# A quantized layer: GpSimd rounds gate, sigmoid and half of act, TensorE spreads the largest value

## The reference

```python
def act_qdq(x):                       # 16 bits, one step for the whole tensor
    qmax = 2.0 ** 15 - 1.0
    scale = jnp.maximum(jnp.max(jnp.abs(x)) / qmax, 1e-12)
    return jnp.clip(jnp.round(x / scale), -qmax - 1.0, qmax) * scale

def fixed_qdq_u16(x):
    scale = 1.0 / 65536.0
    return jnp.clip(jnp.round(x / scale), 0.0, 65535.0) * scale

x = act_qdq(x)
up = act_qdq(x @ lpbq_dequant(w_up).T)        # weights: 4 bits in blocks of 32
gate = act_qdq(x @ lpbq_dequant(w_gate).T)    # 1024 x 768
sig = fixed_qdq_u16(jax.nn.sigmoid(gate))
gate = act_qdq(gate * sig)                    # "act"
o = act_qdq(gate * up)                        # "hid"
return o @ lpbq_dequant(w_down).T
```

## Time and profile before

| | |
|---|---|
| three runs | 4011.01, 4022.51, 4026.56 us (median 4022.51) |
| profiled execution | 4017.75 us, its span 4016.4 us |
| TensorE busy | 3686.9 us, 92% of the span |
| VectorE | 2754.8 us, 69% |
| ScalarE | 2149.5 us, 54% |
| GpSimd | 1459.3 us, 36% |
| the stage of the change | about 830 to 969 us of the span |

### The profile page before, as it was taken

One profiled execution on the slowest core, in us unless ns is written; L12 is line 12 of the kernel. 1 busy time (PEld: TensorE's weight loads), 2 busy tenths in 40 slices (PEclk: granted clock), 3 DMA queues, 4 the chain that ended last, 5 costly groups with the idle time before them and its releaser, 6 DMA issues. The chain is left out here.

```text
span 4016.4 us, 100168 instructions
## 1 busy us (share of the span) xinstructions
PE 3686.9 (92%) x42032; PEld 3196.3 (80%) x42032; DVE 2754.8 (69%) x7205; ACT 2149.5 (54%) x2963; POOL 1459.3 (36%) x1261
## 2 busy tenths in 40 slices
PE   7999999874999999988999999985988999999857
PEld 6888888643888888857788888864987888888646
DVE  5777777665777777753788888854446777777544
ACT  4566565454656656533455555533644656566444
POOL 3333333101322322130665555414763323222146
PEclk9999999997999999999999999986998999999978
DMA  3122123001111111010211121003542111110035
GB/s 99 51 67 59 51 65 115 25 17 37 47 39 35 42 43 35 10 41 10 79 66 59 51 67 59 26 13 105 204 139 75 35 35 46 39 35 26 13 116 176
DMA packets 125584, 235.80 MB, mean 59 GB/s; under 512 B 9920, under 2 KB 114768, under 8 KB 121296
## 3 DMA queue, kind: packets, MB, share of 16 engines
q1 hardware_dynamic: 118032, 175.58, 14.8%
q0 software_dynamic: 7104, 53.81, 3.8%
HBM read 208.39 MB, written 20.97 MB: 57 GB/s over the span
## 5 line engine op out<-in xcount | busy, mean ns | idle before, releaser
L610 ACT COPY prob_t<-ps 128x1024 f32<-128x1024 f32 x512 | 518.0, 1012 | 1037.3 <-PE ps L498 1037.3
L498 PE MATMUL ps<-c_ident,prob 128*128 128x128 f32 (+1 forms) x6656 | 902.5, 277 | 13.7 <-ACT prob L748 9.9
L498 PEld LDWEIGHTS ps<-c_ident,prob 128*128 128x128 f32 (+1 forms) x6656 | 734.7, 141 | 148.0 <-issue 121.5
L748 ACT ACTIVATE prob<-prob,nmx 128x1601 f32<-128x1601 f32 x512 | 828.8, 1626 | 1.1 <-DVE nmx L661 1.1
L528 PE MATMUL ps<-wv,ctx 128*128 128x256 f32 x4992 | 703.6, 289 | 3.1 <-DVE vals L620 3.1
L514 PE MATMUL ps<-ctx,wk 128*128 128x400 f32 (+1 forms) x3072 | 691.0, 360 | 7.4 <-POOL ctx L810 3.4
L528 PEld LDWEIGHTS ps<-wv,ctx 128*128 128x128 f32 x4992 | 618.7, 186 | 10.0 <-DVE vals L620 4.0
L514 PEld LDWEIGHTS ps<-ctx,wk 128*128 128x128 f32 x3072 | 535.2, 191 | 16.5 <-issue 4.9
L652 DVE CUSTOM_DVE_ANT_0 prob<-ps,mk 128x400 f32<-128x400 f32 (+2 forms) x1024 | 525.8, 569 | 32.4 <-PE ps L486 25.2
L655 DVE TENSOR_SCALAR_CACHE_REDUCE prob<-ps 128x400 f32<-128x400 f32 (+2 forms) x1024 | 525.4, 570 | 11.4 <-PE ps L486 8.9
L682 DVE SCALAR_TENSOR_TENSOR keys<-ps,cols,keys 128x400 fp32r<-128x400 f32 (+2 forms) x384 | 243.6, 634 | 367.7 <-ACT keys L754 360.5
(11 more groups left out here) (352 smaller groups left out, 4242.2 us busy)
## 6 DMA issues: line engine op xcount, KB each, us to landing
raw_ctx<-in_ctx_t SPq DMA_DIRECT2D x120, 400.0 KB, 3.3
raw_ctx<-in_ctx_t SPq DMA_DIRECT2D x60, 402.0 KB, 5.1
raw_ctx<-in_ctx_t SPq DMA_DIRECT2D x60, 399.0 KB, 3.3
mk<-in_mask_f SPq DMA_DIRECT2D x32, 400.2 KB, 5.5
mk<-in_mask_i SPq DMA_DIRECT2D x16, 800.5 KB, 4.4
sorted<-zeros SPq DMA_DIRECT2D x2, 3840.0 KB, 20.2
rows<-sorted SPq DMA_DIRECT2D x30, 256.0 KB, 6.8
done<-done SPq DMA_DIRECT2D x30, 256.0 KB, 2.1
```

The costliest lines, as they stand in the source:

```text
L498: mm = pe.transpose(ps[0:w, turn_bank(u, i) + a, r * P:(r + 1) * P], prob[u % 2][:, r, x * P:x * P + w], cst['ident'][:])
L610: copy(prob_t[0:w, place(2 * i):place(2 * i) + nb, :], ps[0:w, turn_bank(u, i):turn_bank(u, i) + nb, :]).then_inc(st[sem], 1)
L748: a.activation(prob[h % 2][:, r, :], prob[h % 2][:, r, :], ACT.Exp, bias=nmx[:, r:r + 1], accum_out=den[h % 2][:, r:r + 1]).then_inc(st['e ...
```

## The change

The change rewrites who does what in the gate and act sections:

- the integers of gate, now with the step multiplied in (`rounded_rows`), are made by GpSimd for all six tiles, those of act for the odd tiles;
- the second pass of the sigmoid's rounding (`sigmoid_rounded`) is GpSimd's; VectorE keeps the first, and runs one tile ahead: it does the first pass of tile m, then the product and the reduction of tile m-1;
- the products of act with up are GpSimd's for the odd tiles, VectorE's for the even ones;
- the largest over partitions comes from a transpose on TensorE of one column spread over 128 (`spread_largest`), whose row VectorE reduces; `step_size` is split in `step_begun` and `step_made`, and for up the quantization of the down weight stands between the two;
- ScalarE's scalings of up come one tile later among its copies of gate.

```diff
             elif old[0] == 'act':
-                engine.wait_ge(*st.at('hidden', old[1] + 1))
+                engine.wait_ge(*hidden(old[1]))
...
+        def spread_largest(n):
+            pe.wait_ge(*st.at('step_big', names.index(n) + 1))
+            pe.transpose(ps[:, 3, 0:P], one[n][:, 0:1].broadcast_to([P, P]), k.cst['ident'][:]).then_inc(st['step_all'], 1)
...
         for m in range(NF):
             project_act(k, st, gate[:, m:m + 1], (6, 7), 'gate_mm', 'gate_out', first=2 * m)
-            scale_rows('up', m)
+            if m:
+                scale_rows('up', m - 1)
+        scale_rows('up', NF - 1)
         turn(2, 'down')
         for m in range(NF):
             scale_rows('gate', m)
-            integers('gate', m)
             buffer_free(a, ('sig', m))
-            a.wait_ge(*st.at('whole', whole['gate', m]))
-            a.activation(buffer(('sig', m))[:], buffer(('gate', m))[:], ACT.Sigmoid,
-                         scale=one['gate'][:, 2:3]).then_inc(st['sigmoid'], 1)
+            a.wait_ge(*st.at('whole', m + 1))
+            a.activation(buffer(('sig', m))[:], buffer(('gate', m))[:], ACT.Sigmoid).then_inc(st['sigmoid'], 1)
...
+        def rounded_rows(n, m):
+            b = buffer((n, m))
+            p.wait_ge(*st.at('scaled', scaled[n, m]))
+            p.tensor_scalar(b[:], b[:], -BIG, one[n][:, 2:3], ALU.add, ALU.mult).then_inc(st['whole'], 1)
+
+        def sigmoid_rounded(m):
+            sig = buffer(('sig', m))
+            p.wait_ge(*st.at('sig_up', m + 1))
+            p.tensor_scalar(sig[:], sig[:], -BIG / 65536.0, 65535.0 / 65536.0, ALU.add, ALU.min).then_inc(st['sig'], 1)
+
+        for m in range(NF):
+            rounded_rows('gate', m)
+            if m:
+                sigmoid_rounded(m - 1)
+        sigmoid_rounded(NF - 1)
+        for m in range(1, NF, 2):
+            rounded_rows('act', m)
+            p.wait_ge(*st.at('whole', NF + m // 2 + 1))
+            p.tensor_tensor(gate[:, m], buffer(('act', m))[:], up[:, m], ALU.mult).then_inc(st['hidden_pool'], 1)
...
+        def step_made(n):
+            v.wait_ge(*st.at('step_all', names.index(n) + 1))
+            v.tensor_reduce(one[n][:, 1:2], ps[:, 3, 0:P], AX, ALU.max).then_inc(*did.up())
+            v.wait_ge(*did.now())
             v.tensor_scalar(one[n][:, 2:3], one[n][:, 1:2], 1.0 / 32767.0, 1e-12, ALU.mult, ALU.max).then_inc(*did.up())
...
+        for m in range(NF + 1):
+            if m < NF:
+                sig = buffer(('sig', m))
+                v.wait_ge(*st.at('sigmoid', m + 1))
+                v.tensor_scalar(sig[:], sig[:], 0.0, BIG / 65536.0, ALU.max, ALU.add).then_inc(st['sig_up'], 1)
+            if m:
+                v.wait_ge(*st.at('sig', m))
+                v.tensor_tensor(gate[:, m - 1], buffer(('gate', m - 1))[:], buffer(('sig', m - 1))[:],
+                                ALU.mult).then_inc(st['gated'], 1)
+                v.wait_ge(*st.at('gated', m))
+                largest('act', m - 1)
+        step_begun('act')
+        step_made('act')
```

More of the change, by code:

```diff
@@ L1474, in quantized_ffn @@
     quantized = {what: i + 1 for i, what in enumerate(w for w in order if w[0] in ('x', 'up', 'hid'))}
-    whole = {what: i + 1 for i, what in enumerate(w for w in order if w[0] in ('gate', 'act'))}
     tile_of = {'x': xq, 'up': up, 'gate': gate, 'act': gate, 'hid': gate}
@@ L1518, in pe @@
         pe.wait_ge(*st.at('w_turned', 6))
-        project_pe(k, st, turned['gate'], xq, (6, 7), 'gate_mm', 'gate_out')
+        for m in range(NF):
+            for n in range(2):
+                if m:
+                    pe.wait_ge(*st.at('gate_out', 2 * m + n - 1))
+                for c in range(C):
+                    mm = pe.matmul(ps[:, 6 + n, :], turned['gate'][:, c, m * P:(m + 1) * P], xq[:, c, n * 512:(n + 1) * 512],
+                                   start=(c == 0), stop=(c == C - 1))
+                mm.then_inc(st['gate_mm'], 1)
+            if m == 0:
+                spread_largest('up')
         turn(2, 'down')
+        for n in ('gate', 'act', 'hid'):
+            spread_largest(n)
         pe.wait_ge(*st.at('w_turned', 9))
@@ L1545, in turn, with integers @@
                 a.copy(flat[:, 512 * j:512 * j + 512], ps[:, j, :]).then_inc(st['w_turned'], 1)
-        def integers(n, m):
-            a.wait_ge(*st.at('scaled', scaled[n, m]))
-            a.activation(buffer((n, m))[:], buffer((n, m))[:], ACT.Identity, bias=minus_col[:]).then_inc(st['whole'], 1)
+        def integers(m):
+            a.wait_ge(*st.at('scaled', scaled['act', m]))
+            a.activation(buffer(('act', m))[:], buffer(('act', m))[:], ACT.Identity, bias=minus_col[:]).then_inc(st['whole_act'], 1)
         a.wait_ge(*st.at('ln_var', 1))
@@ L1574, in act @@
                 if n == 'hid':
-                    a.wait_ge(*st.at('hidden', m + 1))
+                    a.wait_ge(*hidden(m))
                 scale_rows(n, m)
-                if n == 'act':
-                    integers(n, m)
+                if n == 'act' and m % 2 == 0:
+                    integers(m)
     def pool():
         p = nc.gpsimd
-        for i, n in enumerate(names):
-            p.wait_ge(*st.at('step_big', i + 1))
-            p.partition_all_reduce(one[n][:, 1:2], one[n][:, 0:1], P, RMAX).then_inc(st['step_all'], 1)
+        def rounded_rows(n, m):
[6 more added lines that the diff above has]
+            p.tensor_scalar(sig[:], sig[:], -BIG / 65536.0, 65535.0 / 65536.0, ALU.add, ALU.min).then_inc(st['sig'], 1)
+        for m in range(NF):
+            rounded_rows('gate', m)
[6 more added lines that the diff above has]
+            p.tensor_tensor(gate[:, m], buffer(('act', m))[:], up[:, m], ALU.mult).then_inc(st['hidden_pool'], 1)
     def dve():
@@ L1614, in dve @@
                             apply_absolute_value=True).then_inc(*did.up())
-        step_size('x')
+        step_begun('x')
+        step_made('x')
         for c in range(C):
@@ L1629, in dve @@
             largest('gate', m)
-        step_size('gate')
-        for m in range(NF):
-            sig = buffer(('sig', m))
-            v.wait_ge(*st.at('sigmoid', m + 1))
-            v.tensor_scalar(sig[:], sig[:], 0.0, BIG / 65536.0, ALU.max, ALU.add).then_inc(*did.up())
-            v.wait_ge(*did.now())
-            v.tensor_scalar(sig[:], sig[:], -BIG / 65536.0, 65535.0 / 65536.0, ALU.add, ALU.min).then_inc(*did.up())
-            v.wait_ge(*did.now())
-            v.scalar_tensor_tensor(gate[:, m], buffer(('gate', m))[:], one['gate'][:, 2:3], sig[:], ALU.mult,
-                                   ALU.mult).then_inc(st['gated'], 1)
-            v.wait_ge(*st.at('gated', m + 1))
-            largest('act', m)
-        step_size('act')
-        for m in range(NF):
-            v.wait_ge(*st.at('whole', whole['act', m]))
-            v.scalar_tensor_tensor(gate[:, m], buffer(('act', m))[:], one['act'][:, 2:3], up[:, m], ALU.mult,
-                                   ALU.mult).then_inc(st['hidden'], 1)
-            v.wait_ge(*st.at('hidden', m + 1))
+        step_begun('gate')
+        step_made('gate')
+        for m in range(NF + 1):
[3 more added lines that the diff above has]
+                v.tensor_scalar(sig[:], sig[:], 0.0, BIG / 65536.0, ALU.max, ALU.add).then_inc(st['sig_up'], 1)
+            if m:
+                v.wait_ge(*st.at('sig', m))
[5 more added lines that the diff above has]
+        step_made('act')
+        for m in range(NF):
+            if m % 2 == 0:
+                v.wait_ge(*st.at('whole_act', m // 2 + 1))
+                v.scalar_tensor_tensor(gate[:, m], buffer(('act', m))[:], one['act'][:, 2:3], up[:, m], ALU.mult,
+                                       ALU.mult).then_inc(st['hidden'], 1)
+            v.wait_ge(*hidden(m))
             largest('hid', m)
-        step_size('hid')
+        step_begun('hid')
+        step_made('hid')
         for m in range(NF):
```

16 lines of the change are left out of this document (10 added, 6 removed).

## The result

| | before | after |
|---|---|---|
| runs, median (lowest to highest) | 4020.8 us (4010.8 to 4026.56), 7 runs | 4035.88 us (4032.44 to 4044.95), 7 runs |
| profiled execution's span | 4016.4 us | 4033.8 us |
| GpSimd busy | 1459.3 us | 1500.3 us |

The ratio is 1.0047, with a 95% interval of 1.0036 to 1.0059: 15 us slower, beyond the interval but within the 0.5% (20 us) that the prediction took as the border. The forecast was 4044 us, the range 4026 to 4062.

A forecast was written before the change was run, and what follows sets the result against it. Between the last gate product and the output product, VectorE and ScalarE were taken to set the pace. 18.2 + 3.7 + 0.6 + 1.8 - 2.4 = +21.9 us on 4017.75 gave 4039.7, 4044 on the runs' median; range 4026 to 4062.

The forecast's parts named there:

- The ring: Gate section: rotating buffers close a chain of waits, four laps of 7.3 us; section 46.9 us against 28.7, +18.2.
- the signs named: Gate section 47 us, clipping 1.4 us or more, ScalarE waiting at scalings, GpSimd's tensor_scalar 1.9 to 2.0; act section 21.
- the rival without a hold: GpSimd passes at 1.95 us overlap VectorE freely; gate section +14.0, act +0.9, in all +15, 4037 us; chance 0.13.
- I take 1.95 us: Price of each GpSimd tensor_scalar at 1024 columns, from the mask's row less an odd-width cost; lower end 1.04, upper 2.73.
- the mask's row: GpSimd's mask tensor_scalar in the profile before, 4270 ns at 1601 columns, taken as nearest price for the new passes.
- The cheap rival: GpSimd passes at 1.04 us: gate section +8.3, act -1.8, in all +6.5, 4029 us; chance 0.12.
- the dear one: Rival with GpSimd passes at 2.73 us: gate section +27.7, act +6.1, in all +34, 4056 us; chance 0.28.
- The hold: VectorE's tensor_scalar and two-input products don't overlap GpSimd's passes, reductions do; the clipping waits until GpSimd's 1.95 us pass ends.
- The act section: GpSimd's three odd tiles, 3 x (1.95 + 2.36), with VectorE's products between: 21.1 us against 17.4, +3.7.
- The steps: Largest over partitions by transpose and reduction: +0.35 us each for gate, act and hidden, -0.47 for x; +0.6 in all.
- The tail: Ahead of the gate section: two scalings follow the last copy, so VectorE does a second rounding and reduction pair, +1.8 us.
- The next stage: Start of the next layer: no reconfiguring instruction delays GpSimd's first product, -2.4 us, between 0 and -2.9.

The follow-up runs named there:

- opening the ring: The changed kernel with eight rotating buffers in place of four; gate section 42.25 us against 48.27, profiled execution 4039.9 us.
- the fast pass: The changed kernel with multiplication by 1 for min in GpSimd's second sigmoid rounding, upper clamp left out; gate section 36.07 us against 48.27.
- both together: The changed kernel with eight buffers and multiplication by 1 in place of min; gate section 30.06 us against 48.27, profiled execution 4020.59 us.
- the runs with 1023 and with 1600 columns: Changed kernel, GpSimd's rounding cut into columns 1 and 1023: gate section 49.79 us; kernel before, mask's lone multiplication at 1600 columns: 4.27 us.
- the mask in four forms: Kernel before, GpSimd's mask pass as it is (4.28 us), with addition of 0 (1.56), split at 1600 columns (4.27) or 1024 (2.78); 4019.42 us profiled.
- the transpose alone: Kernel before with only the largest over partitions by TensorE transpose and VectorE reduction; 4022.08 us against 4021.5, ratio 1.0001.
- the recast kernel: Kernel before plus the transpose, eight buffers, scaling one tile ahead, one cheap GpSimd pass under VectorE's reduction, fewer VectorE passes; 4008.19 us against 4021.5, ratio 0.997.

## Why the prediction came out as it did

*The ring, the reason for the result, was right.* Four closed laps through product, scaling and both GpSimd passes were forecast at 7.3 us, and measured 7.46; the section at 46.9, measured 48.3; +18.2 against +19.6. Three runs confirm the mechanism: opening the ring gives 6.0 us, the fast pass 12.2, both together their sum. ScalarE's wait for the product at each scaling from tile 2 on was among the signs named, and came.

*That the number came so near was luck in good part.* Of the other signs named in the prediction, two for the gate section failed: GpSimd's tensor_scalar was not at 1.9 to 2.0 us, and VectorE's clipping did not last 1.4 us or more but 0.69. Inside the section the errors also cancel: ahead of the ring it was 7.2 us for the 8.95 forecast, behind it 11.2 for 8.7. The total would not have told: 4035.88 lies nearer to the rival without a hold (4037) than to the forecast, just outside the forecast's own 4036 to 4052. And "slower", which the prediction held likeliest at 0.55, is by its own border of 20 us not what came; "same" had 0.43.

*GpSimd's price was wrong, and the errors cancelled.* The first step that failed is "I take 1.95 us" for every tensor_scalar, reached by taking an odd width out of the mask's row; the runs with 1023 and with 1600 columns show that the oddness was worth nothing, and the mask in four forms that its lone operation was. The rounding with a multiplication measured 1.12 us, the one with min 3.63: 4.75 together, where 3.9 stood in the sum. The cheap rival was right about the first pass and the dear one too low about the second. The Trainium skill (GPSIMD Engine Reference, "Engine selection") calls one-input operations roughly line-rate there; this case agrees for (add, multiply) at 1.09 ns a column, where VectorE's reduction takes 1.19, and neither for min or max (3.5) nor for a single multiplication (2.7).

*The hold was right where two fast operations meet, and wrong beside the min pass.* This is the second step that failed. In the forecast's lap the clipping waited for the second rounding and added 0.69. In truth the sigmoid and the clipping ran beside it, 1.06 + 0.69 us under 3.63. Of 4.75 - 3.9 = +0.85 by the price and -0.69 by the hold the lap came out 0.16 longer. It is the lap of the rival without a hold, at the measured prices: 1.12 + 3.63 + 1.23 + 1.24 + 0.25. Elsewhere the hold is in the rows: 3.45 and 2.19 for a product of 1.29, 2.15 and 2.08 for a rounding of 1.12, 1.50 for a clipping of 0.69.
The Trainium skill (SBUF — State Buffer, "Who interferes with whom") says that whoever starts first has the shared ports for its whole instruction. This case agrees for GpSimd's product and its multiplication; for the min pass it doesn't: VectorE was held 0.9 of 3.73 us, and the measurement decides.

*The act section:* +3.7 forecast, +1.5 measured. The term "3 x (1.95 + 2.36)" has 1.12 for 1.95, which is -2.5. The sign was right, and moving it back gives the 1.5. The cheap rival, with GpSimd's rounding priced about right (1.04) but no hold in it, had -1.8 here.

*The steps:* +0.6 forecast, +0.74 measured (+0.41 three times, x -0.49). *The tail:* +1.8 forecast. The gate step began 63.82 us into the stage against 62.06, +1.76 with the 0.49 of x already in it; so the tail is 2.25, or 1.89 against the transpose alone, which has the change's steps (61.93). *The next stage:* -2.4 forecast, -3.4 measured, against an upper end of -2.9. The reference was the third layer's start at 6.91 us; here it became 6.15. Over all runs without partition_all_reduce the stage took 736.1 to 737.3, so the size is known to about a us.

*The sum.* +21.9 forecast, +20.7 in the two stages, +15 in the medians. The last gap of 5 us is not explained. It is of the size by which untouched stages differ between executions (the fourth layer's cross-attention took 730.4 to 737.5 us over these kernels); the recast kernel shows one of the same sign, the transpose alone does not.

## What to carry to other kernels

Price an operation on GpSimd by the pair of operations in it before scaling by width: here (add, multiply) on 128x1024 was 1.1 us, (add, min) 3.6, a multiplication alone 2.8. Before moving a pass to an idle engine, draw the lap through the rotating buffers with it in; an engine that is 64% idle is still late if its pass stands between two others. In these runs GpSimd's help did no harm only as one cheap pass a tile, issued ahead and released so that it falls on VectorE's reduction; it gained nothing by itself that a run shows. Read a sum's terms against the rows even when the total comes out.

## What the hardware showed that was not expected

- A GpSimd tensor_scalar with a second operation that does nothing (addition of 0) is 2.7 times as fast as the one without it: 1.56 against 4.28 us at 1601 columns.
- min and max as second operation cost 3.62 us at 1024 columns, multiply 1.04 and 1.12; the bound as a constant or from a column makes no difference (3.63, 3.70).
- The slow min or max pass holds VectorE's product for its first 0.8 to 0.9 us only (three places), though a product that came first held such a pass for about as long (4.66 us against 3.63).
- With partition_all_reduces before it, the last 36 us ago, GpSimd's first product of the next stage started 977.53 - 971.32 = 6.2 us behind the layer norm's first instruction; without any, 977.16 - 975.49 = 1.7. The next stage was 2.2 to 3.4 us shorter in the runs without them.
